# Masking every second key tile on GpSimd instead of TensorE in a one-core decoder layer

## The reference, cut to what matters

```python
q = query @ wq.T + bq; k = key @ wk.T + bk; v = value @ wv.T + bv      # query: layernorm(x); key, value: the context
...
scores = jnp.einsum('bhqd,bhkd->bhqk', q, k) / math.sqrt(D_HEAD)
scores = jnp.where(mask == 0, jnp.float32(-1000000000.0), scores)
attn = jax.nn.softmax(scores, axis=-1)
out = jnp.einsum('bhqk,bhkd->bhqd', attn, v)
```

## Time and profile before

| | |
|---|---|
| median of 3 runs | 2957.96 us (2955.64 to 2958.58) |
| profiled execution, its own time | 2953.11 us |
| its span, first to last instruction | 2951.3 us |
| busy share of the span: PE, DVE, ACT, POOL | 93%, 75%, 60%, 53% |
| mean granted clock of TensorE | 0.972 of full speed |

### The profile page before, as it was taken

The page is one execution under the profiler, slowest core; times in us unless marked ns, Lnnn a source line. Parts: engine busy times, 40 slices in busy tenths (PEclk is TensorE's granted clock), DMA queues, the critical chain, the costliest instruction groups (busy, mean ns, idle before and its releaser), DMA issues. The chain is left out here.

```text
span 2951.3 us, 55361 instructions
## 1 busy us (share of the span) xinstructions
PE 2742.2 (93%) x19289; PEld 1814.1 (61%) x19330; DVE 2215.5 (75%) x3289; ACT 1760.7 (60%) x2899; POOL 1559.6 (53%) x853
## 2 busy tenths in 40 slices
PE   5999999999999999999999849999999999999995
PEld 2777777777777777777777634445454545454423
DVE  3988888888888888888888757484848484747463
ACT  5778777877877787778777413534444444444341
POOL 1888888888888888888889631111111111111010
PEclk9999999999999999999999979999999999999988
DMA  3122212212121222122113071414050505050500
GB/s 115 33 72 76 68 53 70 88 33 80 68 76 41 72 76 69 52 75 83 36 64 101 1 164 35 68 27 72 23 77 18 93 2 93 2 93 2 78 9 8
DMA packets 113338, 174.50 MB, mean 59 GB/s; under 512 B 15216, under 2 KB 88048, under 8 KB 113040
## 3 DMA queue, kind: packets, MB, share of 16 engines
q1 hardware_dynamic: 113088, 171.34, 22.7%
HBM read 148.38 MB, written 22.94 MB: 58 GB/s over the span
## 5 line engine op out<-in xcount | busy, mean ns | idle before, releaser
L1066 POOL TENSOR_TENSOR hC<-h,C_rep 128x1024 f32<-128x1024 f32 x512 | 1204.3, 2367 | 235.3 <-PE y_bank L538 230.5
L924 DVE TENSOR_TENSOR_SCAN h<-dA,pair 128x512 f32<-128x512 f32 x1024 | 1178.5, 1204 | 159.1 <-PE pair L447 145.1
L677 ACT ACTIVATE dA<-delta,cols 128x511 f32<-128x511 f32 x1024 | 666.0, 712 | 98.3 <-DVE h L924 93.1
L447 PEld LDWEIGHTS pair<-diagB,duT 64*128 64x128 f32 x8192 | 497.9, 187 | 236.0 <-issue 185.0
L447 PE MATMUL pair<-diagB,duT 64*128 64x128 f32 x8192 | 595.9, 285 | 17.6 <-DVE h L924 8.8
L538 PE MATMUL y_bank<-ident,hC 128*128 128x128 f32 x4120 | 563.3, 280 | 13.7 <-POOL hC L1066 11.8
L538 PEld LDWEIGHTS y_bank<-ident,hC 128*128 128x128 f32 x4120 | 441.9, 141 | 79.9 <-POOL hC L1066 19.7
L1775 DVE CUSTOM_DVE_ANT_0 masked<-pair,mask_bias 128x512 f32<-128x512 f32 x512 | 322.0, 687 | 30.7 <-PE pair L1296 15.0
L1846 POOL TENSOR_SCALAR rstd<-mv 128x4 f32<-128x4 f32 x24 | 11.7, 486 | 567.8 <-DVE mv L1635 567.8
L1528 ACT ACTIVATE pr<-pair 128x1024 f32<-128x1024 f32 x256 | 248.7, 1022 | 94.0 <-PE pair L1296 83.7
L447 PE MATMUL general<-xnT,w_in 128*128 128x512 f32 x512 | 251.8, 603 | 7.4 <-ACT zs L677 5.2
(11 more groups left out here) (174 smaller groups left out, 3146.1 us busy)
## 6 DMA issues: line engine op xcount, KB each, us to landing
C_rep<-c_rows SPq DMA_DIRECT2D x128, 512.0 KB, 3.7
w_in<-w_in SPq DMA_DIRECT2D x16, 1024.0 KB, 4.9
qk_parts<-qk_part SPq DMA_DIRECT2D x48, 256.0 KB, 2.5
k_st<-qk_parts SPq DMA_DIRECT2D x48, 256.0 KB, 8.8
q_st<-qk_parts SPq DMA_DIRECT2D x48, 256.0 KB, 8.9
x_in<-x SPq DMA_DIRECT2D x18, 512.0 KB, 5.4
w_out<-w_out SPq DMA_DIRECT2D x17, 512.0 KB, 4.3
mid<-x_out SPq DMA_DIRECT2D x9, 512.0 KB, 6.4
```

The costliest lines, as they stand in the source:

```text
L447: return pe.matmul(o, lhsT, rhs, start=start, stop=stop)
L677: return act.activation(o, i, fn, **kw)
L924: last = dve.tensor_tensor_scan(h[:, g % 4, i, :], dA[:, g % 4, i, :], dBu[:, i, :], 0.0, ALU.mult, ALU.add)
L1066: pool.tensor_tensor(hC[:, g % 2], h[:, g % 4], C_rep[:, 2 * j:2 * j + 2, :], ALU.mult).then_inc(s_hC.sem, 1)
```

## The change

In each unit the second key tile (`t == 1`) gets no mask product. Instead POOL multiplies the exponentials of that tile by 1 or 0, in place in `pr`, with both read as 32-bit integers, two heads (128 x 2 x 512) at a time (`mask_exp`). `weigh` half 1 waits for POOL's second such operation of its unit, and half 0 for the exponentials as before. The words come from one more DVE operation in the setup. POOL's `rstd_of(ATT, b + 1)`, which stood before the stage, stands after unit 3. `oT` takes the memory of `xT[1]`, which makes room for the words.

```diff
-    oT = sb("oT", [P, 2, T])
+    oT = xT[1]
+    keep_word = sb("keep_word", [P, 2, T], i32)
...
                         kt = 2 * s + t
-                        mm(pair[hh % 2][:, t, :], k_st[0:QR, hd, kt * P:(kt + 1) * P], q_st[0:QR, hd, :], True, False)
-                        last = mm(pair[hh % 2][:, t, :], ident_bf[:, :], mask_biasT[:, kt, :], False, True)
+                        on_pool = t == 1
+                        last = mm(pair[hh % 2][:, t, :], k_st[0:QR, hd, kt * P:(kt + 1) * P], q_st[0:QR, hd, :], True, on_pool)
+                        if not on_pool:
+                            last = mm(pair[hh % 2][:, t, :], ident_bf[:, :], mask_biasT[:, kt, :], False, True)
...
-                pe.wait_ge(s_exp.sem, s_exp.count(b * 2 * H + unit * 4 + 3))
+                if half == 0:
+                    pe.wait_ge(s_exp.sem, s_exp.count(b * 2 * H + unit * 4 + 3))
+                else:
+                    pe.wait_ge(s_kept.sem, s_kept.count(b * H + unit * 2 + 1))
...
+            dve.drain()
+            dve.tensor_scalar(keep_word[:, :, :], mask_biasT[:, 1::2, :], 0.0, None, ALU.is_equal).then_inc(s_word.sem, 1)
...
+            def mask_exp(b, unit, half):
+
+                kt = 2 * (unit % 2) + 1
+                pool.wait_ge(s_exp.sem, s_exp.count(b * 2 * H + unit * 4 + 2 * half + 1))
+                settle(pool)
+                words = pr[:, 2 * half:2 * half + 2, kt, :].bitcast(i32)
+                pool.tensor_tensor(words, words, keep_word[:, unit % 2, :].unsqueeze(1).broadcast_to((P, 2, T)), ALU.mult).then_inc(s_kept.sem, 1)
...
                 for i in range(2):
                     cut_maxima(b, i)
-                if more:
-                    rstd_of(ATT, b + 1)
+                for unit in range(H // 2):
+                    for half in range(2):
+                        mask_exp(b, unit, half)
+                    if more and unit == 3:
+                        rstd_of(ATT, b + 1)
                 rstd_of(FF2, b)
```

More of the change, by code:

```diff
@@ L1197, in attention_pass @@
     s_exp = stage("exp", ahead=2)
+    s_kept = stage("masked_exp")
+    s_word = stage("mask_words")
     g_out = stage("g_out")
@@ L1894, in _ @@
             rstd_of(FF1, 1)
+            def mask_exp(b, unit, half):
[4 more added lines that the diff above has]
+                pool.tensor_tensor(words, words, keep_word[:, unit % 2, :].unsqueeze(1).broadcast_to((P, 2, T)), ALU.mult).then_inc(s_kept.sem, 1)
+            pool.wait_ge(s_word.sem, s_word.count(0))
             def batch(b, more):
```

## The result

The changed kernel takes **3067.33 us** (median of 4 runs, 3057.39 to 3076.81) against 2956.80 of the kernel before on the same chips (2954.30 to 2958.58): ratio 1.0377, 95% interval 1.0360 to 1.0394. The forecast was slower, 3080, with 2970 to 3200 as its range. The profiled execution took 3063.39 us, with a span of 3061.5: 110.2 more than before's 2951.3.

What follows compares the result with a forecast made beforehand. PE was taken to bound the stage before; after the change, POOL's and DVE's turns. Seven batches at 16 us plus 10 for the last make 122 us: 3075 profiled, 3080 us as median, range 2970 to 3200 (0.80).

Steps and rivals of the forecast that it cites:

- A product alone: One 1024-wide integer product on POOL takes 2.35 us, 2.4 with the wait between two of them.
- the rival with the slower integer product: POOL's products take 3.0 us each, giving 3145 us, or 4.7 each, giving near 3350; chance 0.15.
- Products 1 to 8: POOL's products in a batch up to unit 3; the eighth ends at +25.5, or +27.5 with the clock.
- The clock term: PE's half clock after its wait at `weigh` costs PE up to 3.1 us, of which 2 reach POOL.
- the milder loss: No clock loss, luckier DVE order or shorter PE wait: 3057, or 3020 with 2.0 us products; 2970 to 3050; chance 0.15.
- `xn_q` in four pieces: On DVE after `rstd` at +29.0, each piece behind one POOL product, ending at +38.8.
- `tmp`, `mem`, `cnt` of step 2: Three DVE operations in turns with POOL, 3.35 us each, ending at +48.8.
- From `spk` of step 2 to the end of `finish`: DVE: `spk` behind product 16 ends at +51.6, then DVE is alone and `finish` ends at +63.0.
- The store and ACT's wait: Store takes 3.0 us from issue to landing plus 0.5 for waits, +66.5; ACT's `project_k` waits for it.
- Up to the `on` conversions: ACT's `on` conversions end at +69.9 instead of +54.0; each batch with a successor loses 16 us.
- The last batch: The products themselves end late, +54 against the last exponential at +44 before: 10 us.
- PE's 4.2 us wait at the first `weigh`: At unit 0's `weigh` PE stands 4.2 us for POOL's products, with a clock of 0.5 after it.

Runs made afterwards that it cites:

- experiment 5: Changed kernel with the wait for the store's landing moved from ACT's `qk` to DVE, where DVE next writes that buffer; 3060.70 us, ratio 1.0345.
- 5b: Changed kernel with the store's wait moved from ACT to DVE, and `normalise(2)` ahead of `step(4)` in DVE's queue; 3043.80 us, ratio 1.0294.
- experiment 7: Kernel before with only `oT` at the address of `xT[1]` and the setup operation for the words, no POOL products; 2958.28 us, ratio 1.0007.
- experiments 3 and 4: Each against the changed kernel: first, `rstd_of(ATT)` ahead of the products, 3076.09 us; second, without steps 2 to 4 of the spiking neurons, 2973.68 us.
- experiment 1: Changed kernel without POOL's products, so odd key tiles get no mask, and `rstd` ahead of the stage; 2919.04 us, ratio 0.9871.
- the run with 6 products: Changed kernel with POOL products only in units 2, 4 and 6, other mask products on PE, `rstd` ahead; 2937.38 us, ratio 0.9934.

## Why the prediction was right, point by point

The direction, the cause and the size hold: slower, by DVE's and POOL's turns, 3067 against 3080. One link had the wrong name, and some errors cancelled. Step by step, for batch 1, forecast and then measured:

- A product alone 2.35 and paced at 2.4, measured 2.34 and 2.41; in turns 3.35, measured 3.2 to 3.35. Right, and the rival with the slower integer product falls.
- Products 1 to 8 end: +27.5, measured +25.0. **The clock term was put in every batch and belongs in some.** In batch 1 POOL ran without a gap and the 2 us didn't exist. In batch 6 it did, and there the end is +27.5, and `finish` +61.9. Of the seven batches four (1 to 4) end at +25.0, two at +26.3 and one at +27.5. So in four batches a case happened that I had given to the milder loss: the clock costs POOL nothing. Its price was worked out wrongly besides: 16 less the 2 of the clock is 14 per batch, not 13, and its 3057 stood outside its own 2970 to 3050.
- `xn_q` in four pieces: 9.8 us, measured 7.52. Here a turn was too dear: I charged four whole products, and the four pieces lie among three. Its end was forecast for +38.8 and is +33.9.
- `tmp`, `mem`, `cnt` of step 2: 10.0 us, measured 9.8 from the first's start to the last's end. Right.
- From `spk` of step 2 to the end of `finish` 11.4, measured 12.8: `tmp` of step 3 still met product 16 (2.08 instead of 1.23). `finish` +63.0, measured +59.4.
- The store and ACT's wait 3.5, measured 3.3; the conversions 3.4, measured 3.3. The sizes are right, **the role is not**: I had the store as a link and PE as covered at this point. Experiments 5 and 5b show that PE, standing for `normalise(2)` behind `finish` (3.3 us) and then at half clock, was as late as the store's landing. That both ends fall together is luck of the forecast: the number was right with the wrong link.
- Up to the `on` conversions 15.9 per batch, measured 12.1 in batch 1: of the 3.8 between, 2.5 are products 1 to 8, 2.3 `xn_q`, and the end of the steps gives 1.4 back; 0.4 is in small parts. The periods give 13.2 on the mean, mostly since the batches of the other kinds have their `finish` 1.2 to 2.5 us later.
- The last batch 10, measured 9.7 at its `on` conversions (from +51.6 to +61.3), and 2.7 in the tail, where PE ran at half clock.
- Setup and `oT` nothing: no cost that can be told (experiment 7).
- The sum 122, measured 110.2: 112 - 92.2 = 19.8 too much in the batches, 2.4 too little for the last one with the tail, and the 5.6 of the start that I did not have. The last two made good 8 of the 19.8 by luck.

PE's 4.2 us wait at the first `weigh` was forecast with half clock behind it. The traces show both orders. PE's waits in batch 1, and the clock of its start:

```profile
1989.28 0.39 PE L1299 MATMUL pair<-q_st,k_st 99*128 99x512 bf16 x1 [1.77 <-ACT pr L1536]
...
1999.31 1.07 PE L1299 MATMUL general<-pr,v_sb 128*32 128x512 f32 x8 [1.11 <-POOL pr L1912]
...
1988.00:1990.00 2.00, 0.72 (x3) 0.21 (x3) 1.92 (x2) 1.99 (x3) 1.72 (x2) 1.00 0.00 0
1990.00:1992.00 2.00, 1.71 (x6) 0.49 (x6) 1.93 (x2) 2.00 (x3) 1.86 (x2) 0.73 0.00 0
1992.00:1994.00 2.00, 2.00 (x9) 0.51 (x11) 1.92 (x2) 1.11 (x3) 1.67 (x2) 0.50 0.01 2
```

The clock fell to the lower of its two levels (1.2 GHz) before PE ever came to POOL's wait; the slower PE then reached `weigh` so late that 1.11 us of it were left. In batch 6 it is as forecast:

```profile
2787.04 1.94 PE L1299 MATMUL general<-pr,v_sb 128*32 128x512 f32 x8 [3.93 <-POOL pr L1912]
...
2776.00:2778.00 2.00, 0.89 (x4) 0.28 (x5) 1.92 (x2) 2.00 (x3) 1.87 (x2) 1.00 0.00 0
...
2788.00:2790.00 2.00, 2.00 (x11) 0.43 (x4) 0.00 (x0) 0.00 (x0) 2.00 (x2) 0.50 0.00 0
```

The Trainium skill (GPSIMD Engine Reference, Instruction dispatch) gives about 2.5 cycles per element as the floor of a two-input GpSimd operation, set by its one read port; the estimate from it is 2.1 us for 1024 elements. The trace has 2.34, and 2.35 for the float operation, so the measured time decides. The kind of arithmetic isn't part of that floor, and this the runs bear out: the integer product costs what the float one does.

## What to carry to other kernels

Where two engines take turns, count their work as one queue, and ask for which end of that queue the rest waits. Here `finish` breaks even with the kernel before at some 47 us behind the first exponential (a period of 144.7 less the 97.7 behind it), and POOL's last product at 43 to 46 (less the 102 and 98.5 of experiments 3 and 4). Both are estimates for this order of the queues: with `normalise(2)` earlier only 95.4 us stand behind `finish`. Well below these points work given to POOL pays. Above them a microsecond costs about a microsecond, in every batch with a successor: `finish` at +50.3, +59.4 and +62.4 goes with periods of some 147, 157 and 160 us. So it is amount and place that decide on such an offload: 16 products cost 111 us, 8 of the same, spread so that POOL all but keeps up with PE, gain 21. And a wait that the trace names as the last to end (the store's landing) need not be a link: take it away on its own, and look at what is as late.

## What the runs showed of the hardware that I had not expected

- **Nearly the same start of a stage goes two ways in the clock.** In batch 1 of the changed kernel PE was busy for 1.46 and 0.72 us of two stretches of 2 us, and the clock fell to 0.73 and 0.50 in the next two. In batch 1 of experiment 5 it was busy for 1.52 and 0.66 at the same place, and the clock stayed at 1.00 for eight more us, until PE had stood 3.9 us at `weigh` (stretches of experiment 5 below). `finish` came 2.5 us later in the second course. The traces don't show what decides.

```profile
1985.00:1987.00 2.00, 0.66 (x3) 0.21 (x3) 1.92 (x2) 1.99 (x3) 1.73 (x3) 1.00 0.00 0
...
1993.00:1995.00 2.00, 0.00 (x0) 0.00 (x0) 1.93 (x4) 0.75 (x1) 2.00 (x2) 1.00 0.00 0
1995.00:1997.00 2.00, 0.65 (x4) 0.20 (x8) 0.96 (x6) 0.00 (x0) 2.00 (x2) 0.63 0.00 0
```

- **Less work on PE lowered its clock.** Without the mask products the clock fell at the start of the stage in each of the first seven batches and took some 1.05 us of each one's 7.0 (experiment 1). It stayed at 1.00 there in the kernel before, and in the run with 6 products, which keeps the first two units as they were.
- **What escapes the turns.** `x_out` of `normalise`, which takes one of its inputs from PSUM, took 0.62 us for its four pieces at 2035.29, while POOL's last two products ran without a gap until 2037.00, and 0.62 us as well at 2048.09, where POOL was idle. `spk`, with one input and both ends in SBUF, took 2.82 instead of 0.69. PSUM isn't the only way out: the layernorm statistics, which read 256 elements from SBUF and write 6, took 1.40 us for four beside a product at 1997.12, against 1.41 before with POOL idle.
